# First feed-forward: two images summed and squared on other engines, GpSimd scales all; second: ScalarE's first round out of its loop

## The reference

```python
x = x + L0(_gn(x), ...)   # group norm of 8 groups, w1, relu, w2: a feed-forward over channels
x = x + L1(_gn(x), ...)   # four sweeps: new row = row + relu(conv1d(previous row, 9 taps) + bias)
x = x + L2(_gn(x), ...)   # four sweeps without bias
x = x + L3(_gn(x), ...)   # linear attention (8 heads), then o1, gelu, o2: a feed-forward
```

```python
m = jnp.mean(g, axis=(2, 3, 4), keepdims=True)
s = jnp.var(g, axis=(2, 3, 4), keepdims=True)
return ((g - m) / jnp.sqrt(s + eps)).reshape(v.shape)
```

## Time and profile before

| | |
|---|---|
| median of 3 runs | 2723.24 us (2722.13 to 2723.75) |
| profiled execution | 2722.5 us, its span 2720.6 us, granted TensorE clock 0.981 |
| TensorE busy | 2563.4 us, 94% of the span |
| VectorE busy | 1866.0 us, 69% |
| ScalarE busy | 1238.3 us, 46% |
| GpSimd busy | 159.3 us, 6% |
| loading x and the first norm | 0 to about 60 us |
| first feed-forward | about 60 to 155 us |
| eight sweeps | 161 to about 2443 us |
| attention products | about 2449 to 2642 us |
| second feed-forward | 2642 to 2716 us, the last store lands with the span |

### The profile page before, as it was taken

One profiled execution on the slowest core, in us unless ns is written; L12 is line 12 of the kernel. 1 busy time (PEld: TensorE's weight loads), 2 busy tenths in 40 slices (PEclk: granted clock), 3 DMA queues, 4 the chain that ended last, 5 costly groups with the idle time before them and its releaser, 6 DMA issues.

```text
span 2720.6 us, 115694 instructions
## 1 busy us (share of the span) xinstructions
PE 2563.4 (94%) x45062; PEld 2447.6 (90%) x45062; DVE 1866.0 (69%) x6022; ACT 1238.3 (46%) x2502; POOL 159.3 (6%) x275
## 2 busy tenths in 40 slices
PE   2889999999999999997899999999999999959999
PEld 1279999999999999997899999999999999959973
DVE  7976666666566666678666666666666666777875
ACT  1656664222233333356666632222333334566768
POOL 1420000000000000000000000000000000003434
PEclk9999999999999999999899999999999999989989
DMA  6720001222400000023900012223000000240005
GB/s 259 179 73 0 0 0 32 62 60 60 104 0 0 0 5 0 0 62 103 373 22 0 0 39 62 61 60 96 0 0 0 0 0 0 77 108 2 3 14 235
DMA packets 158375, 146.46 MB, mean 54 GB/s; under 512 B 22497, under 2 KB 146018, under 8 KB 154210
## 3 DMA queue, kind: packets, MB, share of 16 engines
q1 hardware_dynamic: 146432, 142.65, 17.9%
q10 hardware_dynamic: 11874, 2.90, 0.5%
HBM read 61.61 MB, written 50.33 MB: 41 GB/s over the span
## 4 chain that ended last, share of the span: by engine, by line
PE 88%; DVE 3%; issue 3%; DMA 3%; ACT 2%; SPq 1%; ACTq 0%; POOL 0%; DVEq 0%
PE banks L719 80%; PE banks L773 4%; PE banks L785 1%; DVE state L915 1%; DMA state<-x_in 1%; PE banks L766 1%; ACT res L481 1%; PE banks L692 1%; DVE state L1023 1%; DMA res<-resid 1%; SPq L262 1%; DMA resid<-state 0%; ACT state L487 0%; POOL state L421 0%; DMA state<-turn_ring 0%
## 5 line engine op out<-in xcount | busy, mean ns | idle before, releaser
L719 PE MATMUL banks<-x_row,w_taps 128*64 128x124 f32 (+2 forms) x40640 | 2201.6, 270 | 14.4 <-DVE x_row L946 8.3
L719 PEld LDWEIGHTS banks<-x_row,w_taps 128*64 128x64 f32 x40640 | 2199.1, 135 | 16.7 <-DVE x_row L946 9.9
L946 DVE SCALAR_TENSOR_TENSOR x_row<-banks,sweep_nbias,biased_row 128x128 f32<-128x128 f32 x2032 | 713.2, 351 | 718.8 <-PE banks L719 702.9
L521 ACT ACTIVATE biased_row<-state,sweep_bias 128x256 f32 (+1 forms) x762 | 512.1, 673 | 1025.6 <-DVE state L949 589.2
L517 ACT ACTIVATE biased_row<-state,aff,gn_a 128x64 f32 (+1 forms) x1016 | 367.0, 432 | 179.3 <-DVE state L955 179.3
L949 DVE SCALAR_TENSOR_TENSOR state<-banks,sweep_nbias,biased_row 128x128 f32 (+1 forms) x1016 | 443.5, 437 | 0.1
L955 DVE SCALAR_TENSOR_TENSOR state<-banks,sweep_nbias,biased_row 128x64 f32 (+1 forms) x1016 | 237.2, 275 | 0.2
L955 DVE SCALAR_TENSOR_TENSOR turn_ring<-banks,sweep_nbias,biased_row 128x64 f32<-128x64 f32 x1016 | 237.3, 276 | 0.0
L407 POOL TENSOR_SCALAR res<-res 128x128 f32<-128x128 f32 x64 | 43.2, 675 | 2395.6 <-ACT res L630 2395.4
L692 PE MATMUL banks<-res,ffn_w 64*64 64x512 f32 x512 | 120.2, 611 | 11.6 <-DVE state L915 10.4
L773 PEld LDWEIGHTS banks<-kvw_s,state 64*128 64x128 f32 x1024 | 118.0, 308 | 0.1
(11 more groups left out here) (123 smaller groups left out, 780.4 us busy)
## 6 DMA issues: line engine op xcount, KB each, us to landing
state<-turn_ring SPq DMA_DIRECT2D x512, 64.0 KB, 1.9
state<-x_in SPq DMA_DIRECT2D x16, 1024.0 KB, 20.8
resid<-state SPq DMA_DIRECT2D x64, 256.0 KB, 3.7
res<-resid SPq DMA_DIRECT2D x16, 1024.0 KB, 8.9
res<-resid SPq DMA_DIRECT2D x32, 512.0 KB, 6.0
resid<-state SPq DMA_DIRECT2D x16, 1024.0 KB, 10.6
out_y<-state SPq DMA_DIRECT2D x16, 1024.0 KB, 3.9
state<-resid SPq DMA_DIRECT2D x32, 256.0 KB, 8.5
```

The lines of the kernel that those rows point to most:

```text
L521: nc.scalar.activation(as_cells(n, biased_row[:, k, :, :]), cells(n, slice(0, B), i, k, g), ACT.Identity, bias=sweep_bias[:, n:n + 1]).the ...
L719: last = nc.tensor.matmul(out_ps[blk, :, lo:hi], w_taps[:, n % 2, s, blk], x_row[c][src][:, :, s + lo:s + hi], start=at == 0, stop=at == T ...
L946: nc.vector.scalar_tensor_tensor(x_row[c][par][:, :, 2:2 + HALF], ps, nb, br, ALU.max, ALU.add).then_inc(row_ready[c], 1)
```

## The change

It has three parts. In layer 0 the tiles of images 2 and 3 (`SUMMED`), from chunk 1 on, are added by a `scalar_tensor_tensor` that also leaves their sum, and ScalarE squares them one round later, between its tiles, with the mean of the first chunk as shift; their mean and variance are made from both sums and from the first chunk's own statistics. GpSimd scales all four images in layer 0. And the first round (the first three in layer 0) is written out ahead of ScalarE's loop, in both layers. The diff, with the calls of the tail:

```diff
+    SUMMED = (2, 3)
...
+        first_tile = sb("first_tile", [P, 2, 2])
+        ffn_squares_summed = sem("ffn_squares_summed")
...
-                    for b in range(1, B):
+                    for b in range(layer, B):
                         pool.wait_ge(ffn_up_done, base + j * B + b + 1)
...
-                with act.Fori(0, CHUNKS) as j:
+                def scale(j):
+                    xs = tile_of(j, 0)
+                    nc.scalar.activation(xs, xs, ACT.Identity, scale=a1[:, 0:1], bias=cb[:, 0:1]).then_inc(x_scaled, 1)
+
+                def square(j, b):
+                    act.wait_ge(ffn_added, j * B + b + 1)
+                    act.wait_ge(shift_ready, 1)
+                    if not isinstance(j, int) or j > 1:
+                        act.wait_ge(ffn_squares_summed, j * 2 + (b - 5))
+                    nc.scalar.activation(sq[:, b - 2, 0:NT].rearrange("p (r w) -> p r w", w=WH), tile_of(j, b), ACT.Square,
+                                         bias=minus_shift[:, b:b + 1], accum_out=sums[:, 1, b, bass.ds(j, 1)]
+                                         ).then_inc(ffn_squares_summed, 1)
+
+                def chunk(j, squares):
                     tile(j, 0)
                     tile(j, 1)
-                    xs = tile_of(j, 0)
-                    nc.scalar.activation(xs, xs, ACT.Identity, scale=a1[:, 0:1], bias=cb[:, 0:1]).then_inc(x_scaled, 1)
+                    if layer:
+                        scale(j)
+                    if squares:
+                        square(j + -1, 2)
                     tile(j, 2)
+                    if squares:
+                        square(j + -1, 3)
                     tile(j, 3)
+
+                chunk(0, False)
+                if layer == 0:
+                    chunk(1, False)
+                    chunk(2, True)
+                with act.Fori(1 if layer else 3, CHUNKS) as j:
+                    chunk(j, layer == 0)
+                if layer == 0:
+                    for b in (2, 3):
+                        square(CHUNKS - 1, b)
...
-                    act.wait_ge(shift_ready, layer + 1)
+                    act.wait_ge(shift_ready, layer + 2)
...
+                def add(j, b, summed):
+                    if layer and b == 0:
+                        dve.wait_ge(x_scaled, j + 1)
+                    else:
+                        dve.wait_ge(x_scaled_by_pool, j * (B - layer) + (B * CHUNKS * layer + b + 1 - layer))
+                    dve.wait_ge(ffn_down_done, j * B + (base + b + 1))
+                    xs = tile_of(j, b)
+                    ps = bank[B + b].rearrange("p (r w) -> p r w", w=WH)
+                    if summed:
+                        nc.vector.scalar_tensor_tensor(xs, ps, 1.0, xs, ALU.mult, ALU.add,
+                                                       accum_out=sums[:, 0, b, bass.ds(j, 1)]).then_inc(ffn_added, 1)
+                        return
+                    nc.vector.tensor_tensor(xs, ps, xs, ALU.add).then_inc(ffn_added, 1)
+                    if with_stats:
+                        dve.wait_ge(ffn_added, j * B + (base + b + 1))
+                        nc.vector.bn_stats(stats[:, b, j, :], xs).then_inc(dve_link, 1)
...
+                for b in range(B):
+                    add(0, b, False)
+                chain[0] += B
+                dve.wait_ge(dve_link, chain[0])
+                for b in SUMMED:
+                    ins = nc.vector.bn_aggr(mv[:, b, :], stats[:, b, 0, :])
+                link(ins)
+                nc.vector.tensor_scalar(minus_shift[:, 2:4], mv[:, 2:4, 0], -1.0, None, ALU.mult).then_inc(shift_ready, 1)
+                link(nc.vector.tensor_scalar(first_tile[:], mv[:, 2:4, :].rearrange("p b s -> p s b"), 1.0 / CHUNKS, None, ALU.mult))
+                with dve.Fori(1, CHUNKS) as j:
                     for b in range(B):
...
+                        add(j, b, b in SUMMED)
+                chain[0] += (CHUNKS - 1) * (B - len(SUMMED))
+                dve.wait_ge(dve_link, chain[0])
+                for b in range(B):
+                    if b not in SUMMED:
+                        nc.vector.bn_aggr(mv[:, b, :], stats[:, b, :, :].rearrange("p j s -> p (j s)"))
+                dve.wait_ge(ffn_added, B * CHUNKS)
+                dve.wait_ge(ffn_squares_summed, len(SUMMED) * (CHUNKS - 1))
+                means = gn_t[:, 2:4, 2:4]
+                link(nc.vector.tensor_reduce(means, sums[:, :, 2:4, 1:CHUNKS], axis=AX.X, op=ALU.add))
+                link(nc.vector.scalar_tensor_tensor(means, means, 1.0 / (CR * HALF * CHUNKS), first_tile[:], ALU.mult, ALU.add))
+                nc.vector.tensor_copy(mv[:, 2:4, 0], gn_t[:, 2, 2:4])
+                link(nc.vector.tensor_tensor(gn_t[:, 0, 2:4], gn_t[:, 2, 2:4], minus_shift[:, 2:4], ALU.add))
+                link(nc.vector.tensor_tensor(gn_t[:, 0, 2:4], gn_t[:, 0, 2:4], gn_t[:, 0, 2:4], ALU.mult))
+                to_pe(nc.vector.tensor_tensor(mv[:, 2:4, 1], gn_t[:, 3, 2:4], gn_t[:, 0, 2:4], ALU.subtract))
...
-            from_bn_stats()
             for layer in range(2):
                 group_norm()
```

More of the change, by code:

```diff
@@ L906, in ffn @@
                 base = B * CHUNKS * layer
-                with dve.Fori(0, CHUNKS) as j:
-                    for b in range(B):
[L909 to L919, removed]
@@ L920, in ffn @@
-                if with_stats:
-                    chain[0] += CHUNKS * B
-                    dve.wait_ge(dve_link, chain[0])
+                def add(j, b, summed):
[14 more added lines that the diff above has]
+                        nc.vector.bn_stats(stats[:, b, j, :], xs).then_inc(dve_link, 1)
@@ new lines, in ffn @@
+                if not with_stats:
+                    with dve.Fori(0, CHUNKS) as j:
+                        for b in range(B):
+                            add(j, b, False)
+                    return
+                for b in range(B):
[6 more added lines that the diff above has]
+                nc.vector.tensor_scalar(minus_shift[:, 2:4], mv[:, 2:4, 0], -1.0, None, ALU.mult).then_inc(shift_ready, 1)
```

## The result

The changed kernel takes 2691.32 us (median of four runs, 2690.28 to 2696.16), against 2723.49 before: a ratio of 0.9886, 95% interval 0.9869 to 0.9903 (the two medians alone divide to 0.9882). That is 32.2 us less; 35.0 were forecast, and 2691.3 lies in the likeliest case's own range of 2683 to 2692. A second set of runs gave 2692.28, just outside it.

The account below looks back on a forecast made before the run. The prediction took VectorE to bound the first feed-forward and ScalarE the second. 20.9 less 1.5 for the stores, plus 15.6, made 35.0 us: 2722.5 to 2687.5, 2688.2 at the median's level; 8-in-10 range 2682 to 2697.

Parts of the forecast that it names:

- likeliest case: Whole kernel: the forecast itself, likeliest time 2688 us, own range 2683 to 2692; chance 0.68, including nothing lagging in the stores.
- One load left: Second feed-forward, ScalarE: one table load in round 0, none in 15 rounds; rounds fall from 4.44 to TensorE's 3.44 us.
- start, 0.8: Second feed-forward, round 1: without the load, the down product of image 0 starts at 2648.81, 0.8 us earlier.
- An addition with a sum follows itself after 0.61 also from PSUM: First feed-forward, VectorE: addition with accumulator taken at 0.61 us, as on SBUF operands, making VectorE's round 4.08.
- Squares at 0.75: First feed-forward, ScalarE: each square with its sum written to SBUF takes 0.75 us, between 0.71 and 1.00.
- The loop of two rounds: First feed-forward: chain through all engines from image 2's addition to itself two rounds later, 8.35 us, 4.18 per round.
- E: First feed-forward: the end of the last addition, 154.61 before the change and forecast at 133.7, 20.9 us earlier.
- Rival B: First feed-forward: squares at 1.00 and two slower hand-overs make rounds of 4.6, 6.3 us less gain, 2694 us; chance 0.12.
- Once, 1.4 us: First feed-forward, after round 0: VectorE's two aggregations, two small operations and three links delay round 1's first addition 1.4 us.
- The stores lag by 1.5: First feed-forward: 15 stores, at 4.4 us each if that is a floor, fall behind 1.5 us in all, between 0 and 3.3.
- Rival A: First feed-forward: the stores are the bound, each holding the queue 4.9 us, 15 lagging 10.8; time 2697 us, chance 0.13.
- The norm's tail: End of first feed-forward: the norm's last operations reach TensorE 2.6 us after E, no later than before; worth 0.

## Why the prediction was right, and where it was off

- *VectorE bounds the first feed-forward before, ScalarE the second, TensorE neither.* Right: each part of the change acts on its own stretch only, and GpSimd's scaling alone changes nothing.
- *One load left, rounds of 3.44 set by TensorE, 1.00 won per round.* Right to the hundredth: 4.44 and 3.43 measured. The term "start, 0.8" failed: from the first up product to the first down product of round 1 are 7.20 us before and 7.62 after, 0.4 more and not 0.8 less. I took the first round as it was and did not ask where the load would be put. It moved behind a wait, 1.2 us onto the path. 15.6 forecast, 14.4 measured; the run with the load ahead has 6.45 at the start and 15.6 in all.
- *An addition with a sum follows itself after 0.61 also from PSUM; VectorE's own round is 4.08.* Right: 4.08 with the squares late.
- *Squares at 0.75.* 0.70 to 0.73.
- *The loop of two rounds sets the round, 8.35 us.* The mechanism is right (cutting it gives 4.08), the size was 8.83. Two links were too short: addition to square, 0.75 forecast and 0.98 measured, and the two products with the hand-over behind them, 1.92 forecast and 2.25 measured. The first is the loop's form: written out it is 0.72. The second is so in part, 2.12 with both loops written out; the other 0.2 is the price of the products themselves, taken too short. From the first addition of round 1 to E this makes 65.7 us where 62.7 were forecast: 3.0, the largest error. The round, 4.39 to 4.41, lies just outside the 4.1 to 4.3 that the prediction named as its sign. Rival B named the hand-overs, with 4.6 because it also took the squares at 1.00.
- *Once, 1.4 us.* Measured 0.6 (first addition to that of round 1: 5.75 before, 6.36 after): an aggregation over one chunk's statistics is 0.13 us, not 0.47.
- *The stores lag by 1.5, between 0 and 3.3.* 0.7 to 0.9 at rounds of 4.39. At 4.08 it is 3.5, which is 15 times 0.23: the 4.4 us per store that the prediction took as a floor were nearly right (4.08 + 0.23 = 4.3). Rival A's 4.9 is out.
- *The norm's tail is worth 0.* Right: its product starts at E + 2.3, 2.6 forecast, 2.85 before, and nobody waits for it until the store is off the path.
- The sum of the errors: 3.0 + 1.2 less won, 0.8 + 0.8 more, 2.6 in all: 35.0 forecast, 32.4 measured by the stretches. That the total came so near is in part luck: two terms were forecast too dear and gave back 1.6 of the 4.2 us that two others were forecast too cheap.

## What to carry to other kernels

When the bounding engine is relieved, sum the chain through all in-order queues and not only each engine's own work: here VectorE had 4.08 us of work per round, ScalarE 3.7, TensorE 3.4, and the round was 4.41. A link that stands behind a wait in a hardware loop cost 0.1 to 0.3 us more here than its written-out form, and asking for side work one round later took it out of the loop entirely. The stores, hidden at a share of 0.77 before, still kept up at rounds of 4.39 us and no longer at 4.08, so look first at whether anyone needs all of a transfer so early.

## What was not expected of the hardware

- In ScalarE's loop a square started 0.99 us after the addition that it waits for, written out 0.72, with the same waits in both; what differs is that the loop works out counts and addresses in registers. On VectorE bn_stats behind its addition went from 0.82 to 0.70 when written out.
- The one table load left stood where its activation stands, behind that one's wait (2632.54, after the first up product of 2630.58); with the loop over all rounds it stood at the head and ran during the wait (2642.55).
- Two bn_aggr take 0.25 us together over 6 elements each, and 1.03 over 96.
- While SyncE lagged behind the additions, its issue of one part took up to 1.57 us instead of 0.63, and the DMA share stayed at 0.92, not 1. Why an issue takes longer is not shown: the kernel before has one of 1.59 too, in its first store.
